# A graph network in one kernel: message terms as the weights of the source sums, and two transfers of the first layer issued at other places

## The chip, the core and the metric

The kernel runs on one core of a Trainium2 chip. The core has five engines with instruction streams of their own: TensorE (PE, with its weight loads shown as PEld), VectorE (DVE), ScalarE (ACT), GpSimd (POOL) and SyncE (SP), which issues most of the DMA transfers. They wait for one another through semaphores. The metric is device time in microseconds; lower is better.

## What is computed

A graph has 6250 nodes with 128 features and 106250 directed edges, sorted by destination (50000 random pairs in both directions and one loop for each node). The reference, cut to what matters:

```python
h = relu(layernorm(x))
for W_l, W_r, b in layers:                      # two layers
    agg = segment_sum(h[src], dst) / max(count, 1)
    h = relu(agg @ W_l + h @ W_r + b)
x = x + h
h = relu(layernorm(x))                          # third stage
m = relu(concat(h[src], h[dst]) @ W_interact + b_interact)
m = segment_sum(m, src) / 4
out = x + relu((h + m) @ W_update + b_update)   # the last x is the middle sum
```

## The kernel before

**Start, to about 128 us.** The edges are read, the layer norm is made, and 1250 bins of five destination nodes each are filled from the edge list. `t_rows` in DRAM receives the features of all nodes as two float16 terms (a high and a low one, 512 bytes a row).

**First layer, about 128 to 560 us.** The count matrix of edges is built in 16 slabs of 320 destination nodes. One slab has 16 units. For each unit DVE makes two one-hot tiles (L1843, L1848), PE multiplies them into PSUM (`build`, L1244) and ACT evicts the product into one of two slab buffers (L1023). Between the builds of slab s, PE multiplies the feature table with slab s-1 (`dense_part`, L1255). Of the 16 slabs the first 14 (`STORED`) are also written to DRAM for the second layer (SP, L684), and ACT may not evict slab s before the store of slab s-2, which used the same buffer, has landed. `finish` (L1859) on DVE multiplies a slab's sum by the inverse counts of its nodes, which SP has loaded into `inv` (`load_inv`, L669). Beside this run a histogram of the sources, whose sums DVE takes out of PSUM at slab 2, unit 4 (`blocks_counted`, L1893), and the stages of a sort.

The destinations past node 5120 go another way. POOL gathers the source rows of their edges out of `t_rows` with indirect transfers, eight of 128 rows for each of 20 groups (`fetch_tail`, L898). The row buffer holds 20 transfers: from transfer 20 on, each further eight wait until PE has used an earlier group. PE sums a group at its place in the stream of units (`tail_group`, L1313), and DVE multiplies it by inverse counts from `tail_inv` (L1916) and adds the result (L1813).

**Second layer, about 560 to 900 us**, takes the 14 stored slabs back from DRAM and the last two from their buffers.

**Third stage, about 900 to 1538 us.** The edges are now sorted by source in 50 blocks of 125 nodes, each with 18 tiles of 128 edges, in six groups of three tiles (`GB` = 6, `GT` = 3, 300 groups in all). For each group gi:

- POOL gathers the `b_rows` of nine of the 18 tiles of a block (L934, 9 transfers a block, nine buffers `rows_g`, so up to nine groups ahead);
- DVE makes one-hot tiles three groups ahead (`prepare`, L2215, L2225, L2228);
- PE sums each tile's source and destination part in PSUM bank gi % 4 (`edge_sum`, L1470 and L1479; each is a weight load of 128 columns and a matmul of 128 columns);
- DVE adds the gathered rows into the bank (`add_rows`, L2261);
- ACT writes relu of it as the float16 high term of `msg` (L1155), DVE the low term (`low_term`, L2269);
- four groups later PE sums the messages into their source nodes (`source_sum`, L1490): the one-hot of the sources, 128 edges by 126 columns, is the weights, and both terms of the messages, 256 columns, stream past it. The result of a block is 126 by 256 in PSUM bank 4 + b % 2.

After a block, DVE adds the two halves (`whole_sum`, L2277), PE transposes the sum (`turn_sum`, L1502) and DVE scales it and adds it to `hT` (`keep_sum`, L2283). After every five or so blocks PE multiplies by the update weights (L1510), DVE adds bias and residual (L2290, L2297), and SP stores the output.

**Order around the change.** Everything is in program order on each engine. In the loop over gi, PE runs `source_sum(gi - 4)`, `edge_sum(gi)`, then at group 2 of block b `turn_sum(b - 2)`. DVE runs `add_rows(gi)`, `low_term(gi - 1)`, `prepare(gi + 3)`, then at group 2 `split_lo` and `keep_sum(b - 2)`, at group 4 `whole_sum(b - 1)`. On SP's queue the order was: store of `t_rows[0]` (L656), the fill of `a_rows` with `x` from DRAM to DRAM (L658: 6250 rows of 512 bytes, 125 rows a step, only so that every row is defined before the gathers of the third stage), then for each slab s: at s = 4 `load_tail_inv(0)` (L661), `load_inv(0, s)`, the wait for the eviction of slab s, the store of slab s.

Of the kernel before, what the change touches and what calls it, by code (L numbers as in the profile page):

```python
# [6 lines left out]
def gnn_kernel(nc, x, src, dst, W_l0, W_r0, b0, W_l1, W_r1, b1, W_int, b_int, W_upd, b_upd, out):  # L7
# [5 lines left out]
    ALU = mybir.AluOpType  # L13
    ACT = mybir.ActivationFunctionType
    AX = mybir.AxisListType
    P = 128
    N, D = x.shape
# [34 lines left out]
    STORED = NS - 2  # L52
# [11 lines left out]
    HALVES = 2  # L64
# [16 lines left out]
    BN = 125  # L81
    NB = N // BN
    BE = BN + 1
# [8 lines left out]
    GB = 2 * SIDE  # L92
    GT = TB // GB
# [100 lines left out]
    LAST_BLOCK = [min((c + 1) * CT * P, N) - 1 for c in range(NC)]  # L194
    LAST_BLOCK = [node // BN for node in LAST_BLOCK]
# [7 lines left out]
    with ctx:  # L203
        start = {}
# [8 lines left out]
        def sem(name):  # L213
            return ctx.enter_context(nc.semaphore(name))

        a_rows = nc.dram_tensor("a_rows", [N, D], f32).ap()
# [25 lines left out]
        settle = sb("settle", [P, 1])  # L242
# [28 lines left out]
        ident = sb("ident", [P, P])  # L271
# [11 lines left out]
        scaled = sb("scaled", [P, SC])  # L283
# [5 lines left out]
        ps = ctx.enter_context(nc.psum_tensor("ps", [P, 8, 512], f32))  # L289
# [76 lines left out]
        msg = [x.bitcast(f16).rearrange("p (j k f) -> p j k f", j=GT, k=2) for x in msg_f]  # L366
# [22 lines left out]
        src_hot = [x.bitcast(f16)[:, 0:GT * BE].rearrange("p (j n) -> p j n", j=GT) for x in src_hot_f]  # L389
# [8 lines left out]
        g_b = inv[:, 1, 0:D]  # L398
        g_msg = scaled[:, 0:D]
        g_hot = scaled[:, D:D + BN]  # L400
        block_sum = scaled[:, 0:D]

        s_const = sem("s_const")
        s_iota = sem("s_iota")
# [50 lines left out]
        s_first = sem("s_first")  # L455
# [43 lines left out]
        e_full = sem("e_full")  # L499
        e_msg = sem("e_msg")  # L500
        e_low = sem("e_low")
        e_whole = sem("e_whole")
        e_turned = sem("e_turned")
        e_psum = sem("e_psum")
        e_added = sem("e_added")
        o_lin = sem("o_lin")
        o_biased = sem("o_biased")
# [61 lines left out]
        DECODED_AT = (3, 2)  # L569
# [61 lines left out]
        def _(sp):  # L631
# [13 lines left out]
            for p0, p1 in LAST_ROWS:  # L645
# [9 lines left out]
            sp.wait_ge(PS_[0]["t_lo"], NC)  # L655
            sp.dma_start(t_rows[0].rearrange("(t p) f -> p t f", p=P), table.rearrange("p t k n -> p t (k n)")  # L656
                         ).then_inc(l_store[0], 16)
            sp.dma_start(a_rows.rearrange("(t p) f -> p t f", p=BN), x.rearrange("(t p) f -> p t f", p=BN)  # L658
                         ).then_inc(s_first, 16)
            def load_tail_inv(L):  # L660
                sp.dma_start(tail_inv[L], inv_row[DENSE:ROWS].rearrange("(a n) -> a n", a=1  # L661
                                                                        ).to_broadcast([P, ROWS - DENSE])
# [2 lines left out]
            def load_inv(L, q):  # L665
                if q > 1:
                    sp.wait_ge(AS[L]["scaled"], q - 1)
                s = ORDER[q] if L else q
                sp.dma_start(inv[:, q % 2, :], inv_row[s * SC:(s + 1) * SC].rearrange("(a n) -> a n", a=1  # L669
                                                                                    ).to_broadcast([P, SC])  # L670
                             ).then_inc(s_inv[q % 2], 16)
# [3 lines left out]
                sp.dma_start(slab_rows(slab[q % 2])[:, g, :], slabs_d[ORDER[q], g, :, :]).then_inc(s_land[q % 2][g // 2], 16)  # L675

            for s in range(NS):
                if s == DECODED_AT[0] + 1:
                    sp.wait_ge(AS[0]["hot"], DECODED_AT[0] * SU + DECODED_AT[1] + 2)
                    load_tail_inv(0)  # L680
                load_inv(0, s)
                sp.wait_ge(AS[0]["evict"], min(s * SU + SU, UNITS) + PRE)
                if s < STORED:
                    sp.dma_start(slabs_d[s].rearrange("g p n -> p g n"), slab_rows(slab[s % 2])  # L684
                                 ).then_inc(s_kept[s % 2], 16)
            sp.wait_ge(q_build, BUILT)
            sp.wait_ge(s_irow, 32)
            load_tail_inv(1)
# [53 lines left out]
            for c in range(NC):  # L742
                sp.wait_ge(f_bok, c + 1)
                to = b_rows[c * CB:(c + 1) * CB, :].rearrange("(t p) f -> p t f", p=BN)
# [418 lines left out]
        def _(pe):  # L1163
            t = nc.tensor
# [10 lines left out]
            for h in range(2):  # L1175
                last = t.matmul(ps[:, 4, h * HG:(h + 1) * HG], ones[0:HG, :], diag[:, h, :], start=True, stop=True)
# [31 lines left out]
            for k in range(2):  # L1208
                last = t.matmul(ps[:, 5, 0:1], scaled[:, k * D:(k + 1) * D], ones[:, 0:1], start=k == 0, stop=k == 1)
# [14 lines left out]
            with pe.Fori(0, rounds) as r:  # L1224
                pe.wait_ge(c_five, r + 1)
                for k in range(BW):
                    for j in range(NC):
                        last = t.matmul(ps[:, 4, j * BW + k:j * BW + k + 1], five[:, k, j * P:(j + 1) * P],
                                        ones_b[:, 0:1], start=True, stop=True)
# [253 lines left out]
            def source_sum(gi):  # L1483
                b, g = divmod(gi, GB)
                pe.wait_ge(e_low, gi + 1)
                pe.wait_ge(e_dvehot if g in DVE_HOTS else e_srchot, hots(gi))
                if g == 0 and b > 1:
                    pe.wait_ge(e_whole, b - 1)
                for j in range(GT):
                    last = t.matmul(ps[0:BE, 4 + b % 2, 0:2 * D], src_hot[gi % 6][:, j, :],  # L1490
                                    msg[gi % 3][:, j, :, :].rearrange("p k f -> p (k f)"),
                                    start=g == 0 and j == 0, stop=g == GB - 1 and j == GT - 1)
                last.then_inc(e_psum, 1)

            def turn_sum(b):
                pe.wait_ge(e_whole, b + 1)
                if b:
                    pe.wait_ge(e_added, b)
                updated = sum(last < b for last in LAST_BLOCK)
                if updated:  # L1500
                    pe.wait_ge(o_biased, updated)
                t.transpose(ps[:, 7, 2 * P:2 * P + BN], block_sum[0:BN, :], ident[0:BN, 0:BN]).then_inc(e_turned, 1)  # L1502

            def update(c):
                pe.wait_ge(e_added, LAST_BLOCK[c] + 1)
# [8 lines left out]
            for gi in range(NGR):  # L1514
                b, g = divmod(gi, GB)
                if gi > 3:
                    source_sum(gi - 4)
                edge_sum(gi)
                if gi == GENERAL_AT + AHEAD:
                    general_edges()  # L1520
                if g == 2 and b > 1:
                    turn_sum(b - 2)
                if g == GB - 1 and b - 2 in LAST_BLOCK:
                    update(LAST_BLOCK.index(b - 2))
            turn_sum(NB - 2)
            source_sum(NGR - 4)
            source_sum(NGR - 3)
            source_sum(NGR - 2)
            source_sum(NGR - 1)
            turn_sum(NB - 1)  # L1530
            update(NC - 1)

        @block.vector
        def _(dve):
            v = nc.vector
# [35 lines left out]
            for h in range(2):  # L1571
# [5 lines left out]
                                 op=ALU.min, axis=AX.X))  # L1577
            nc.vector.sem_inc(k_flag, 1)
            dve.wait_ge(s_x[1], 48)
            for t in range(4 * CT, NT):  # L1580
                last = tile_stats(x0, t)
# [44 lines left out]
            def floor_div(to, of, temp):  # L1626
# [9 lines left out]
                                 in1=gbin[:, 1, :].unsqueeze(2).to_broadcast([P, NW, WT]), op=ALU.subtract))  # L1636
            v.tensor_reduce(out=met[:, 0, :], in_=k_rel.rearrange("p (k t) -> p t k", t=WT)[:, :, 0:NW - 1],
                            op=ALU.min, axis=AX.X)
            link(v.tensor_reduce(out=met[:, 1, :], in_=k_rel.rearrange("p (k t) -> p t k", t=WT), op=ALU.max,
                                 axis=AX.X))  # L1640
            link(v.tensor_tensor(out=met[:, 0, 0:WT - 1], in0=met[:, 0, 0:WT - 1], in1=rel_of[:, NW - 1, 0:WT - 1],
                                 op=ALU.min))
# [620 lines left out]

            def low_term(gi):
                dve.wait_ge(e_msg, gi + 1)
                if gi > 2:
                    dve.wait_ge(e_psum, gi - 2)
                to = msg[gi % 3]
                v.scalar_tensor_tensor(out=to[:, :, 1, :],  # L2269
                                       in0=ps[:, gi % 4, 0:GW].rearrange("p (j f) -> p j f", j=GT), scalar=0.0,  # L2270
                                       in1=to[:, :, 0, :], op0=ALU.max, op1=ALU.subtract).then_inc(e_low, 1)

            def whole_sum(b):
                dve.wait_ge(e_psum, (b + 1) * GB)
                if b:
                    dve.wait_ge(e_turned, b)
                v.tensor_reduce(out=block_sum[0:BN, :], in_=ps[0:BN, 4 + b % 2, 0:2 * D].rearrange("p (k f) -> p f k", k=2),  # L2277
                                op=ALU.add, axis=AX.X).then_inc(e_whole, 1)

            def keep_sum(b):  # L2280
                dve.wait_ge(e_turned, b + 1)
                to = hT[:, b * BN:(b + 1) * BN]
                v.scalar_tensor_tensor(out=to, in0=ps[:, 7, 2 * P:2 * P + BN], scalar=settle[:, 0:1], in1=to,  # L2283
                                       op0=ALU.mult, op1=ALU.add).then_inc(e_added, 1)

            def biased(c):
# [17 lines left out]
            for gi in range(NGR):  # L2304
                b, g = divmod(gi, GB)
                add_rows(gi)
                if gi:
                    low_term(gi - 1)
                if gi + AHEAD < NGR:
                    prepare(gi + AHEAD)  # L2310
                    source_hot(gi + AHEAD)
                if gi == GENERAL_AT:
                    general_edges()
                if g == 2 and b + 1 < NB:
                    split_lo(b + 1)
                if g == 2 and b > 1:
                    keep_sum(b - 2)
                if g == 4 and b:
                    whole_sum(b - 1)
                if g == GB - 1 and b - 2 in LAST_BLOCK:  # L2320
                    biased(LAST_BLOCK.index(b - 2))
                if g == 1 and b - 3 in LAST_BLOCK:
                    residual(LAST_BLOCK.index(b - 3))
            low_term(NGR - 1)
            keep_sum(NB - 2)
            whole_sum(NB - 1)
            keep_sum(NB - 1)
            biased(NC - 1)
            residual(NC - 1)
# [22 lines left out]
```

## Time and profile before

| | us |
|---|---|
| median of three runs | 1537.74 (1535.6 to 1540.89) |
| the profiled execution | 1539.85 |
| its span in the profile | 1538.0 |

| engine | busy us | share of the span |
|---|---|---|
| PE | 1326.8 | 86% |
| DVE | 1322.1 | 86% |
| ACT | 939.7 | 61% |
| POOL | 931.3 | 61% |

The shares are averages over stages that have different limits. The profiled execution is 1.85 us longer than its span, and 2.1 us above the median. "Idle" in a row is the time for which the engine did nothing just before the instruction, with what released it. Successive DVE instructions overlap by some hundredths of a microsecond, so the price of one in a dense stream is the distance from its start to the next start, not its duration.

### The profile page before, as it was taken

To read this page: it belongs to the slowest core of one execution; us is meant where nothing else is said; L and a number is where in the kernel's file an instruction comes from. 1 tells how busy PE (TensorE), PEld (TensorE's weight loads), DVE (VectorE), ACT (ScalarE), POOL (GpSimd) and SP (SyncE) were. 2 spreads that over 40 slices of the span, in tenths; PEclk is the share of its full clock that TensorE was granted. 3 is DMA by queue.
4 is the path that set the end of the run, shared out by engine and by line. 5 is a ranking of instruction groups with operands and counts; after the bars stand their busy time and mean duration, and the time that the engine had idled before them with its cause. 6 is when DMAs were issued, how large, how long until landed. Compare 5 with 4: busy or idle time off the path is not lost.

```text
span 1538.0 us, 39495 instructions
## 1 busy us (share of the span) xinstructions
PE 1326.8 (86%) x14762; PEld 1131.1 (74%) x14762; DVE 1322.1 (86%) x3949; ACT 939.7 (61%) x1831; POOL 931.3 (61%) x942
## 2 busy tenths in 40 slices
PE   1426788998999988999999679899999999999997
PEld 1213566776777866777777578889899999998887
DVE  7948797999999845777776779999999999999998
ACT  2646576787778940101001458888878878888886
POOL 5263505887882006677770157777777777777773
PEclk9955899999999999999999789999999999999999
DMA  4005724646473238899996134444445444444542
GB/s 122 0 1 139 287 110 158 242 170 244 154 260 136 103 95 281 279 301 311 301 285 220 30 98 126 120 128 128 121 127 126 124 144 123 131 122 128 128 120 62
DMA packets 121784, 241.62 MB, mean 157 GB/s; under 512 B 20184, under 2 KB 74601, under 8 KB 121594
## 3 DMA queue, kind: packets, MB, share of 16 engines
q1 hardware_dynamic: 95179, 187.74, 36.8%
q0 software_dynamic: 24832, 50.78, 13.5%
q8 instruction: 118, 1.93, 0.5%
q10 hardware_dynamic: 1584, 0.59, 0.2%
q14 instruction: 71, 0.58, 0.1%
HBM read 169.09 MB, written 73.14 MB: 157 GB/s over the span
## 4 chain that ended last, share of the span: by engine, by line
PE 50%; DVE 31%; issue 7%; ACT 4%; DMA 3%; POOL 2%; SPq 1%; ACTq 0%; DVEq 0%; POOLq 0%
PE ps L1273 13%; PE ps L1479 12%; PE ps L1255 6%; DVE room L2225 6%; DVE hot L1848 4%; PE ps L1244 4%; PE ps L1490 3%; PE ps L1470 3%; DVE slab L2269 2%; PE ps L1313 2%; DVE ps L2261 2%; DVE keys L1974 2%; DVE hot L1843 2%; DVE keys L1973 2%; DVE slab L2225 1%
## 5 line engine op out<-in xcount | busy, mean ns | idle before, releaser
L1023 ACT ACTIVATE slab<-ps 128x980 f16<-128x980 f32 x256 | 321.4, 1277 | 111.9 <-PE ps L1244 94.6
L934 POOL DMA_INDIRECT cells<-b_rows,work x236 | 243.3, 1031 | 74.9 <-issue 68.0
L1479 PE MATMUL ps<-slab,room 125*128 125x128 f16 x3538 | 236.0, 221 | 35.2 <-DVE room L2225 32.7
L1255 PE MATMUL ps<-slab,room 128*128 128x320 f16 x1568 | 251.9, 301 | 0.1
L1134 ACT ACTIVATE lnw<-iota_w,keys 128x126 f32<-128x126 f32 x750 | 242.5, 389 | 0.0
L1479 PEld LDWEIGHTS ps<-slab,room 125*128 125x128 f16 x3538 | 206.5, 98 | 48.7 <-DVE room L2225 48.3
L1470 PE MATMUL ps<-inv,hot 125*128 125x128 f16 x1800 | 224.2, 220 | 5.1 <-DVE hot L2215 4.9
L1273 PE MATMUL ps<-slab,room 128*128 128x320 f16 x1568 | 227.1, 301 | 0.0
L1244 PE MATMUL ps<-hot 128*128 128x245 bf16 x1024 | 161.4, 283 | 50.3 <-DVE hot L1848 38.0
L898 POOL DMA_INDIRECT hot<-t_rows,pairs x160 | 165.9, 1037 | 55.4 <-issue 48.2
L1273 PEld LDWEIGHTS ps<-slab,room 128*128 128x128 f16 x1568 | 153.4, 98 | 59.6 <-issue 2.7
L1255 PEld LDWEIGHTS ps<-slab,room 128*128 128x128 f16 x1568 | 153.5, 98 | 47.4 <-issue 1.0
L1479 PE MATMUL ps<-slab 125*128 125x128 f16 x2676 | 179.6, 220 | 2.7 <-DVE slab L2225 2.6
L898 POOL DMA_INDIRECT tslot<-t_rows,pairs x80 | 117.2, 1465 | 95.6 <-PE ps L1313 62.4
L1244 PEld LDWEIGHTS ps<-hot 128*128 128x128 bf16 x1024 | 108.1, 116 | 86.9 <-DVE hot L1848 51.5
L1848 DVE TENSOR_TENSOR hot<-iota_hi,cell_hi 128x984 bf16<-128x984 bf16 x256 | 170.7, 667 | 0.0
L1479 PEld LDWEIGHTS ps<-slab 125*128 125x128 f16 x2676 | 157.0, 98 | 3.8 <-DVE slab L2225 3.5
L1470 PEld LDWEIGHTS ps<-inv,hot 125*128 125x128 f16 x1800 | 144.1, 98 | 10.2 <-issue 5.0
L1973 DVE TENSOR_TENSOR keys<-keys 128x256 f32<-128x256 f32 (+1 forms) x212 | 112.0, 528 | 38.4 <-ACT keys L1006 22.5
L934 POOL DMA_INDIRECT cell_lo<-b_rows,work x115 | 119.8, 1042 | 36.3 <-issue 33.5
L934 POOL DMA_INDIRECT cell_hi<-b_rows,work x99 | 104.9, 1060 | 31.4 <-issue 28.7
L898 POOL DMA_INDIRECT rest<-t_rows,pairs x80 | 104.0, 1300 | 24.9 <-issue 24.1
(376 smaller groups left out, 2418.7 us busy)
## 6 DMA issues: line engine op xcount, KB each, us to landing
slabs_d<-slab SPq DMA_DIRECT2D x14, 3920.0 KB
slab<-slabs_d SPq DMA_DIRECT2D x98, 560.0 KB, 5.3
hot<-lane_d SPq DMA_DIRECT2D x50, 576.0 KB
inv<-inv_row SPq DMA_DIRECT2D x32, 160.0 KB, 6.6
keys<-up_d SPq DMA_DIRECT2D x25, 160.0 KB
room<-up_d SPq DMA_DIRECT2D x25, 160.0 KB
cells<-b_rows,work POOLq DMA_INDIRECT x236
t_rows<-room SPq DMA_DIRECT2D x1, 3200.0 KB, 13.6
```

The source lines that it names most:

```text
L898: p.indirect_dma_start(tail_rows[L][i % RT[L]], None, t_rows[L], bass.IndirectOffsetOnAxis(ap=pairs[:, t, 0:1], axis=0)).then_inc(e_gath[a ...
L934: p.indirect_dma_start(rows_g[gi % RS][:, j, :], None, b_rows, bass.IndirectOffsetOnAxis(ap=node_t[:, t:t + 1], axis=0)).then_inc(e_gath[g ...
L1023: a.activation(slab[par][:, :, u * UB * BW:(u + 1) * UB * BW].rearrange("p h (k d) -> p k h d", k=UB), psum_unit(u).rearrange("p k (h d) - ...
L1134: last = a.activation(far[:, j, :], iota_w[:, 0:BE], ACT.Square, bias=lane_g[:, gi * GT + j:gi * GT + j + 1])
L1244: last = t.matmul(to[:, k, :], lo[:, :, k], hi[:, k, 0:HB], start=True, stop=True)
L1255: last = t.matmul(ps[:, 4 + s % 2, 0:SC], table[:, h, term, :], slab[s % 2][:, h, :], start=k == 0, stop=k == HI * HALVES - 1)
L1273: last = t.matmul(ps[:, 4 + q % 2, 0:SC], table[:, h, term, :], slab[q % 2][:, h, :], start=k == 0, stop=k == HI * HALVES - 1)
L1470: last = t.matmul(to, lanes_of, a_terms[0:BN, b % 2, k, :], start=k == 0, stop=not picked and k == HALVES - 1)
L1479: last = t.matmul(to, end_hot[g // 3][0:BN, u:u + P], bt[0:BN, bt_at(tile, w), k, :], start=False, stop=w == w1 - 1 and k == HALVES - 1)
L1848: v.tensor_tensor(out=hot[:, u % 4, P * UB:(P + HB + 1) * UB].rearrange("p (k w t) -> p k w t", k=UB, t=2), in0=iota_hi[:, :].rearrange("p ...
L1973: v.tensor_tensor(out=new[0], in0=old[0], in1=old[1], op=ALU.max if down else ALU.min)
L2225: last = v.tensor_scalar(to, row, (down_s if h else up_s)[0:BN, w:w + 1], None, ALU.is_equal)
```

## The change

In the third stage the operands of the source sum change places. A message term, 128 edges by 128 features, is the weights, and the one-hot of the sources, 125 columns, streams past it. High and low term go one after the other into the same PSUM columns, so there are six matmuls for a group of three tiles instead of three, and the block's sum comes out as features by nodes, with the two terms already added. `whole_sum`, `turn_sum`, their semaphores and the buffer `block_sum` go. `keep_sum(b)` reads the sum where it is; it stands where `whole_sum` stood (group 4 of block b + 1). `low_term` no longer waits for the source sum three groups back on its own; ACT, whose high term it waits for, still does.

In the first layer the fill of `a_rows` moves from ahead of the slabs to slab 14, behind the wait for that slab's eviction. `load_tail_inv(0)`, which stood ahead of `load_inv(0, 4)`, stands behind `load_inv(0, 3)` and its own wait for slab 3, unit 3, and so ahead of the wait for slab 3's eviction and of its store.

```diff
             sp.wait_ge(PS_[0]["t_lo"], NC)
             sp.dma_start(t_rows[0]. ...).then_inc(l_store[0], 16)
-            sp.dma_start(a_rows.rearrange("(t p) f -> p t f", p=BN), x.rearrange("(t p) f -> p t f", p=BN)
-                         ).then_inc(s_first, 16)
...
             for s in range(NS):
-                if s == DECODED_AT[0] + 1:
+                load_inv(0, s)
+                if s == DECODED_AT[0]:
                     sp.wait_ge(AS[0]["hot"], DECODED_AT[0] * SU + DECODED_AT[1] + 2)
                     load_tail_inv(0)
-                load_inv(0, s)
                 sp.wait_ge(AS[0]["evict"], min(s * SU + SU, UNITS) + PRE)
                 if s < STORED:
                     sp.dma_start(slabs_d[s]. ...).then_inc(s_kept[s % 2], 16)
+                if s == STORED:
+                    sp.dma_start(a_rows.rearrange("(t p) f -> p t f", p=BN), x.rearrange("(t p) f -> p t f", p=BN)
+                                 ).then_inc(s_first, 16)
...
                 if g == 0 and b > 1:
-                    pe.wait_ge(e_whole, b - 1)
+                    pe.wait_ge(e_added, b - 1)
                 for j in range(GT):
-                    last = t.matmul(ps[0:BE, 4 + b % 2, 0:2 * D], src_hot[gi % 6][:, j, :],
-                                    msg[gi % 3][:, j, :, :].rearrange("p k f -> p (k f)"),
-                                    start=g == 0 and j == 0, stop=g == GB - 1 and j == GT - 1)
+                    for k in range(HALVES):
+                        last = t.matmul(ps[:, 4 + b % 2, 0:BN], msg[gi % 3][:, j, k, :], src_hot[gi % 6][:, j, 0:BN],
+                                        start=g == 0 and j == 0 and k == 0,
+                                        stop=g == GB - 1 and j == GT - 1 and k == HALVES - 1)
                 last.then_inc(e_psum, 1)
-            def turn_sum(b):
...
-                t.transpose(ps[:, 7, 2 * P:2 * P + BN], block_sum[0:BN, :], ident[0:BN, 0:BN]).then_inc(e_turned, 1)
...
                 dve.wait_ge(e_msg, gi + 1)
-                if gi > 2:
-                    dve.wait_ge(e_psum, gi - 2)
...
-            def whole_sum(b):
+            def keep_sum(b):
                 dve.wait_ge(e_psum, (b + 1) * GB)
-                if b:
-                    dve.wait_ge(e_turned, b)
-                v.tensor_reduce(out=block_sum[0:BN, :], ...).then_inc(e_whole, 1)
-
-            def keep_sum(b):
-                dve.wait_ge(e_turned, b + 1)
                 to = hT[:, b * BN:(b + 1) * BN]
-                v.scalar_tensor_tensor(out=to, in0=ps[:, 7, 2 * P:2 * P + BN], scalar=settle[:, 0:1], in1=to,
+                v.scalar_tensor_tensor(out=to, in0=ps[:, 4 + b % 2, 0:BN], scalar=settle[:, 0:1], in1=to,
                                        op0=ALU.mult, op1=ALU.add).then_inc(e_added, 1)
...
-                if g == 2 and b > 1:
-                    keep_sum(b - 2)
                 if g == 4 and b:
-                    whole_sum(b - 1)
+                    keep_sum(b - 1)
```

## Rows read from the trace of the kernel before

**Rows 1.** Busy time by engine: us, PE, PEld, DVE, ACT, POOL, PEclk, DMA, GB/s.

```profile
1064.00:1416.00 352.00, 333.60 (x5231) 322.49 (x5228) 350.66 (x1278) 284.08 (x758) 272.75 (x261) 1.00 0.48 127
```

**Rows 2.** Timeline of SP's queue, first layer: start, us, line, transfer.

```profile
125.31 9.47 SPq L658 DMA_DIRECT2D a_rows<-in_x  x1
134.83 33.27 SPq L669 DMA_DIRECT2D inv<-inv_row  x1
```

**Rows 3.** Timeline at the eviction of slab 2; in brackets the idle time ahead.

```profile
182.00 3.67 ACT L1023 ACTIVATE slab<-ps 128x980 f16<-128x980 f32 x3 [9.22 <-DMA slabs_d<-slab]
...
183.40 0.98 PE L1244 MATMUL ps<-hot 128*128 128x245 bf16 x4 [7.68 <-ACT slab L1023]
...
187.42 1.28 DVE L1893 TENSOR_REDUCE share<-ps 128x32 f32<-128x512 f32 x2 [10.03 <-PE ps L1351]
```

**Rows 4.** Timeline at the first tail group of the first layer.

```profile
235.15 0.57 SPq L661 DMA_DIRECT2D cells<-inv_row  x1
...
249.47 0.29 DVE L1916 TENSOR_TENSOR hrow<-ps,cells 128x128 f32<-128x128 f32 x1 [6.22 <-DMA cells<-inv_row]
...
258.32 0.35 DVE L1813 SCALAR_TENSOR_TENSOR hT<-ps,lift,hT 128x128 f32<-128x128 f32 x1 [2.21 <-PE ps L1319]
```

**Rows 5.** Timeline of the tail's gathers on POOL, and PE's use of group 8.

```profile
235.91 3.66 POOL L898 DMA_INDIRECT tslot<-t_rows,pairs  x1 [56.86 <-PE ps L1313]
...
257.09 0.94 POOL L898 DMA_INDIRECT tslot<-t_rows,pairs  x1 [5.51 <-PE ps L1313]
...
339.70 0.95 POOL L898 DMA_INDIRECT rest<-t_rows,pairs  x1 [0.30 <-issue]
...
342.77 0.83 PE L1313 MATMUL ps<-hrow,tslot 128*128 128x128 f16 x12
```

**Rows 6.** DMA queue, 138 to 150 us: packets, MB, share; timeline, layer one's end.

```profile
q1 hardware_dynamic: 2256, 1.15, 32.1%
...
517.50 2.66 ACT L1023 ACTIVATE slab<-ps 128x980 f16<-128x980 f32 x2
...
557.99 0.49 DVE L1859 TENSOR_TENSOR scaled<-ps,inv 128x320 f32<-128x320 f32 x1
```

**Rows 7.** Chain that ended last, one block; a group: busy us, mean ns.

```profile
1219.90 1.00 PE ps L1479 x18
1221.02 0.33 PE ps L1490 x3
...
1222.69 0.12 PE ps L1502
...
L1490 PEld LDWEIGHTS ps<-slab,rest 128*126 128x126 f16 x288 | 31.7, 137 | 1.8 <-DVE slab L2269 1.8
```

**Rows 8.** Timeline of one block of the third stage, PE and DVE.

```profile
1224.98 0.28 PE L1470 MATMUL ps<-inv,hot 125*128 125x128 f16 x2
...
1225.50 0.29 DVE L2261 TENSOR_TENSOR ps<-ps,cells 128x128 f32<-128x128 f32 x1
...
1230.94 0.41 DVE L2277 TENSOR_REDUCE scaled<-ps 125x128 f32<-125x256 f32 x1
...
1231.28 0.42 DVE L2261 TENSOR_TENSOR ps<-ps,cells 128x256 f32<-128x256 f32 x1
```

**Rows 9.** Timeline: gathers of group 0 in blocks 10 and 42, and their use.

```profile
1028.13 1.45 POOL L934 DMA_INDIRECT cell_hi<-b_rows,work  x1 [0.30 <-issue]
...
1033.41 0.30 DVE L2261 TENSOR_TENSOR ps<-ps,cell_hi 128x128 f32<-128x128 f32 x1
...
1416.47 0.94 POOL L934 DMA_INDIRECT cells<-b_rows,work  x1 [0.30 <-issue]
...
1432.34 0.28 DVE L2261 TENSOR_TENSOR ps<-ps,cells 128x128 f32<-128x128 f32 x1
```

**Rows 10.** Timeline of the third stage's end.

```profile
1530.25 0.42 DVE L2277 TENSOR_REDUCE scaled<-ps 125x128 f32<-125x256 f32 x1 [0.38 <-PE ps L1490]
...
1531.10 0.35 DVE L2283 SCALAR_TENSOR_TENSOR hT<-ps,settle,hT 128x125 f32<-128x125 f32 x1 [0.42 <-PE ps L1502]
```

More of the change, by code:

```diff
@@ L400, in gnn_kernel @@
         g_hot = scaled[:, D:D + BN]
-        block_sum = scaled[:, 0:D]
         s_const = sem("s_const")
@@ L501, in gnn_kernel @@
         e_low = sem("e_low")
-        e_whole = sem("e_whole")
-        e_turned = sem("e_turned")
         e_psum = sem("e_psum")
@@ L1487, in source_sum @@
                 if g == 0 and b > 1:
-                    pe.wait_ge(e_whole, b - 1)
+                    pe.wait_ge(e_added, b - 1)
                 for j in range(GT):
-                    last = t.matmul(ps[0:BE, 4 + b % 2, 0:2 * D], src_hot[gi % 6][:, j, :],
-                                    msg[gi % 3][:, j, :, :].rearrange("p k f -> p (k f)"),
-                                    start=g == 0 and j == 0, stop=g == GB - 1 and j == GT - 1)
+                    for k in range(HALVES):
+                        last = t.matmul(ps[:, 4 + b % 2, 0:BN], msg[gi % 3][:, j, k, :], src_hot[gi % 6][:, j, 0:BN],
+                                        start=g == 0 and j == 0 and k == 0,
+                                        stop=g == GB - 1 and j == GT - 1 and k == HALVES - 1)
                 last.then_inc(e_psum, 1)
-            def turn_sum(b):
-                pe.wait_ge(e_whole, b + 1)
-                if b:
[L1498 to L1501, printed above, removed]
-                t.transpose(ps[:, 7, 2 * P:2 * P + BN], block_sum[0:BN, :], ident[0:BN, 0:BN]).then_inc(e_turned, 1)
             def update(c):
@@ L1520, in _ @@
                     general_edges()
-                if g == 2 and b > 1:
-                    turn_sum(b - 2)
                 if g == GB - 1 and b - 2 in LAST_BLOCK:
                     update(LAST_BLOCK.index(b - 2))
-            turn_sum(NB - 2)
             source_sum(NGR - 4)
@@ L1529, in _ @@
             source_sum(NGR - 1)
-            turn_sum(NB - 1)
             update(NC - 1)
@@ L2271, in low_term @@
                                        in1=to[:, :, 0, :], op0=ALU.max, op1=ALU.subtract).then_inc(e_low, 1)
-            def whole_sum(b):
+            def keep_sum(b):
                 dve.wait_ge(e_psum, (b + 1) * GB)
-                if b:
-                    dve.wait_ge(e_turned, b)
-                v.tensor_reduce(out=block_sum[0:BN, :], in_=ps[0:BN, 4 + b % 2, 0:2 * D].rearrange("p (k f) -> p f k", k=2),
-                                op=ALU.add, axis=AX.X).then_inc(e_whole, 1)
-            def keep_sum(b):
-                dve.wait_ge(e_turned, b + 1)
                 to = hT[:, b * BN:(b + 1) * BN]
-                v.scalar_tensor_tensor(out=to, in0=ps[:, 7, 2 * P:2 * P + BN], scalar=settle[:, 0:1], in1=to,
+                v.scalar_tensor_tensor(out=to, in0=ps[:, 4 + b % 2, 0:BN], scalar=settle[:, 0:1], in1=to,
                                        op0=ALU.mult, op1=ALU.add).then_inc(e_added, 1)
@@ L2315, in _ @@
                     split_lo(b + 1)
-                if g == 2 and b > 1:
-                    keep_sum(b - 2)
                 if g == 4 and b:
-                    whole_sum(b - 1)
+                    keep_sum(b - 1)
                 if g == GB - 1 and b - 2 in LAST_BLOCK:
@@ L2324, in _ @@
             low_term(NGR - 1)
-            keep_sum(NB - 2)
-            whole_sum(NB - 1)
             keep_sum(NB - 1)
```

## The prediction, made before the changed kernel ran

> **What bounds the kernel now.** I read busy time by stretch first, then the timeline at the longest waits, then how far each producer runs ahead of its user.
>
> In the middle of the third stage DVE is busy for 350.66 of 352 us and PE for 333.60, so DVE has the least room [rows 1]. POOL looks idle there, 272.75 us of 352, but it issued 261 gathers, and ahead of each stand 0.30 us of issue that aren't counted as busy [rows 1, 9]. 261 times 0.30 is 78, and 273 + 78 is 351 of 352 us: POOL has no room either. Two rows 32 blocks apart give the paces. POOL's first gather of a block starts at 1028.13 in block 10 and at 1416.47 in block 42, 12.14 us a block; DVE's use of it starts at 1033.41 and 1432.34, 12.47 us a block [rows 9]. So POOL's lead grows from 5.3 us to 15.9. The 5.3 us hold the gather's 1.45 us of issue and its landing; up to about block 12 DVE is fed just in time, and only after that is DVE alone the bound.
>
> In the first layer two waits stand out. ACT can't evict slab 2 for 9.22 us, because the store of slab 0 hasn't landed; PE waits 7.68 us behind ACT, and DVE 10.03 us behind PE [rows 3]. The store is late because SP could not issue it: the fill of `a_rows` held SP for 9.47 us, and the load of `inv` behind it for 33.27, until 168.10 [rows 2]. Later DVE waits 6.22 us for `tail_inv`, issued only at 235.15, and 2.21 us more for a PE that had stood still meanwhile [rows 4].
>
> **The change part by part.** *The fill leaves the front.* Without it SP issues the store of slab 0 when the slab is evicted, about 20 us before 168, and it lands before slab 2 asks. `inv`, moved ahead with it, is needed only from slab 2 on. The wait of 9.22 us goes. Between 7.68 (PE's wait) and 10.03 (DVE's) I take 9, nearer to DVE, which works without a gap behind it.
>
> *`tail_inv` earlier.* Its issue moves ahead of the eviction of slab 3, by about a slab (some 20 us). What it is moved past, that eviction's wait and the store of slab 3, isn't held up, since its own wait (slab 3, unit 3) ends long before. DVE's 6.22 us go, and with them the 2.21 of the follow-up: 8.4, at least 6.2. Together 17.4 us.
>
> *What is late next: the tail's gathers.* The gather released by PE's group 0 starts at 235.91; eight take until 251.6 (257.09 less 5.51 of waiting for PE's group 1), and then the stream runs on nearly without a wait to the last gather of group 8, which ends at 340.65, only 2.1 us before PE uses it at 342.77 [rows 5]. With group 0 earlier by 9, its eight gathers end at about 242.6; group 1, earlier by 17, would release the next at about 239, so they follow at once, at 242.9 in place of 257.09. The stream moves by about 14.5, PE wants 17.4, and the 2.1 us are hardly more than a landing. So the first layer gains about 15, not 17.4. Bounds: 18.4 (10.03 + 8.4, gathers keeping up), and about 7.7, if longer gathers beside the slab stores eat half.
>
> *The fill at its new place.* Slab 14's eviction ends at 520.16 [rows 6]. While the fill was alone on SP's queue, that queue moved 1.15 MB in 12 us [rows 6]; 3.2 MB take 33 us, so it ends near 554. Queued behind it on SP are `load_inv(0, 15)`, `load_tail_inv(1)` and the first loads of layer two. The first is the earliest needed: DVE multiplies slab 15 at 557.99 [rows 6]. About 4 us of cover; price 0. Without the cover: the old fill kept SP until 42.8 us after its issue at 125.31 [rows 2], which would be 563.0 here, 5 us late plus a landing, so 8 us at most.
>
> *The source sum on PE.* 18 matmuls with 256 columns a block become 36 with 125. Today three take 0.33 us [rows 7]. Their like in size is the pair of L1479, a load of 128 columns and a matmul of 128: 18 take 1.00 us, 0.056 each [rows 7]. Six are 0.33: PE neither gains nor loses. Below: six at 0.052 (125 of 128 columns) save 0.02 us a group. Above: a pair costs as much as one of today's, 0.11 us. I take 0.056, nearest in shape. The Trainium skill (TensorE: Matmul & The Clock Gate, section Back-to-back issue gap) speaks against the change: in a stream of weight loads and matmuls with 128 columns it puts about 81 ns on each. This trace's 18 in 1.00 us disagree. By the skill's figure the stage would gain almost nothing (third rival).
>
> *`whole_sum` and `turn_sum`.* DVE's slot of L2277 is 0.34 us (1230.94 to the next start at 1231.28) [rows 8], and L1502 holds PE for 0.12 [rows 7]; both go once a block. `keep_sum` keeps its price and moves to the place of `whole_sum`. DVE 12.47 less 0.34 is 12.13, just POOL's 12.14: from block 10 to 42 the lead stays at 5 us instead of growing by 10.6, and that is the gain, with 7 more blocks of 0.34 (2.4): 13. The first ten blocks stay fed by POOL and give nothing. Gathers land unevenly, and a lead that no longer grows can't swallow that; I take off 2: 11. Bounds: 17 (50 times 0.34, POOL no limit) and 8.
>
> *Does PE hold DVE back?* At group 3 PE's sum ends at 1225.26 and DVE uses it at 1225.50: 0.24 us of room [rows 8]. DVE becomes 0.34 faster; the loop from DVE's one-hots over PE back to this point becomes 0.12 faster by L1502. 0.24 + 0.12 - 0.34 leaves 0.02. PE just follows.
>
> *The waits.* `keep_sum(b)` waits for the sum that `whole_sum(b)` waited for, at the same place. `source_sum` at group 0 now waits for `keep_sum` where it waited for `whole_sum`, so the same instruction slot on DVE. The update's wait for `keep_sum` comes a block earlier. `low_term`'s dropped wait was already met by ACT's. All nothing.
>
> *The end.* Behind the last source sum stood L2277 and the transpose; now `keep_sum` can start at 1530.25 in place of 1531.10 [rows 10]: 0.85. With 0.3 for L2277 in the last group, about 1.
>
> **Sum.** 15 + 11 + 1 = 27. Span 1538.0 to 1511, the profiled execution 1539.85 to 1513, the median 1537.74 to 1511.
>
> **Rivals.** *Gathers limit neither stage.* [...] Against: 351 of 352 us. 17.4 + 17 + 1: 1502.
>
> *The gathers take most of the first layer's gain.* For: 2.1 us of lead at group 8. 7.7 + 11 + 1: 1518.
>
> *Pairs with messages as weights cost more than L1479's.* Twelve pairs of two source sums lie in PE's loop between its wait for DVE and group 3. At 0.08 the loop gets 0.29 longer, and of 0.34 a block about 0.05 stays, 2.5 us in all: 15 + 2.5 + 1, 1519. At 0.11 it gets 0.65 longer and costs 0.3 a block: the first layer's gain is gone, 1537. Against: L1479's rows. The skill's 81 ns named above is the milder case.
>
> *The fill at slab 14 isn't covered.* 8 us later than forecast: 1519. For: only 4 us of cover. Against: less other traffic there than in its old place.
>
> *The slower side: the load isn't hidden.* The weights are now the tile written last, `low_term`'s output. If each load, 137 ns for L1490 today [rows 7], stood unhidden ahead of its matmul, the loop's twelve pairs cost 1.64 us more; less the 0.36 of room and transpose, 1.3 a block, 64 in all, against 16 gained: about 1586. It turns slower than before from about 0.11 us a pair on. Against: only the first of a group's six loads waits for a semaphore, and L1479's loads, behind waits on DVE as well, are hidden.
>
> That the change doesn't do what it says is in the third and fifth: DVE's instruction surely goes, and the question is who takes its place.
>
> **How the numbers follow.** Measurement can tell about 0.3% from no change, 4.6 us. Forecast 1511 (1506 to 1516) 0.55; gathers no limit, 1502, 0.12; gathers eat the first layer, 1518, 0.11; fill uncovered, 1519, 0.09; dearer pairs, 1519 to 1537, 0.08, of which 0.03 end near no change; unhidden loads, 1586, 0.03; nothing moves, 0.02. Faster 0.92, same 0.05, slower 0.03. The range 1502 to 1522 takes in the first four.
>
> **What would show it.** Fill: no wait of ACT on `slabs_d`, and SP's long issue at about 500 instead of 135; the multiplication of slab 15 without a wait on `inv`. `tail_inv`: no wait at L1916. Gathers: PE waiting at tail group 8. Source sum: six matmuls in 0.33 us. Third stage: POOL's lead near 5 us at block 42 instead of 15.9, DVE with short waits for gathers throughout, no L2277 and no transpose. I am wrong in a step if PE waits more for DVE than before at L1479 while DVE waits for L1470 (the pairs), or if POOL's pace leaves 12.1 us a block.

## The result, and the profile after

The changed kernel takes 1517.12 us (median of four runs, 1513.23 to 1523.65) where the kernel before takes 1539.32 beside it: 0.985 of before, 95% interval 0.982 to 0.987, which is 24 us less (the two medians differ by 22). The forecast was 27 us less, 1511, with 1502 to 1522 as its range. In a later set of five runs the same kernel stood at 0.983 (0.981 to 0.985). The profiled execution has a span of 1511.4 us against 1538.0, 26.6 less.

The total was near, but its parts were not. Putting the same instruction of both traces side by side, DVE is 17.3 us earlier behind the two stalls, 19.5 from the tenth tail group on, 18.6 at the start of the third stage, 24.8 at its last block and 26.6 at the end. So the first layer gave about 19 (15 forecast), the third stage 6.2 (11 forecast) and the end 1.8 (1 forecast).

First SP's queue in the changed kernel: start, us held, line, transfer. It answers [rows 2] and [rows 6].

```profile
124.12 9.49 SPq L664 DMA_DIRECT2D inv<-inv_row  x1
147.44 0.36 SPq L679 DMA_DIRECT2D slabs_d<-slab  x1
...
500.70 0.93 SPq L682 DMA_DIRECT2D a_rows<-in_x  x1
502.21 27.82 SPq L664 DMA_DIRECT2D inv<-inv_row  x1
530.14 0.35 SPq L656 DMA_DIRECT2D work<-inv_row  x1
```

The store of slab 0 is issued at 147.44 in place of 168.16. The transfer issued behind the fill holds SP's queue for 27.82 us in the new place, as the one behind it did for 33.27 in the old one. The 9.47 us that the prediction gives to the fill were not the fill's: the load of `inv`, which now stands in that place behind the store of `t_rows`, is held for 9.49.

The timeline at the eviction of slab 2, at the first tail group, at tail group 9, and at the multiplication of slab 15 (in brackets the idle time ahead); it answers [rows 3], [rows 4] and [rows 6].

```profile
174.15 3.75 ACT L1021 ACTIVATE slab<-ps 128x980 f16<-128x980 f32 x3 [0.91 <-PE ps L1242]
178.16 1.28 DVE L1879 TENSOR_REDUCE share<-ps 128x32 f32<-128x512 f32 x2 [0.32 <-PE ps L1349]
...
233.91 0.28 DVE L1902 TENSOR_TENSOR hrow<-ps,cells 128x128 f32<-128x128 f32 x1
241.01 0.35 DVE L1799 SCALAR_TENSOR_TENSOR hT<-ps,lift,hT 128x128 f32<-128x128 f32 x1 [0.47 <-PE ps L1317]
...
339.20 1.06 PE L1311 MATMUL ps<-hrow,rest 128*128 128x128 f16 x16
...
538.51 0.49 DVE L1845 TENSOR_TENSOR scaled<-ps,inv 128x320 f32<-128x320 f32 x1
```

ACT's 9.22 us, DVE's 10.03 and 6.22 are gone. Slab 15 is multiplied at 538.51, 38 us behind the issue of the fill and without a wait. The row at 339.20 has a counterpart that the prediction left out. In the kernel before, PE waited 2.02 us ahead of tail group 9:

```profile
358.66 1.05 PE L1313 MATMUL ps<-hrow,rest 128*128 128x128 f16 x16 [2.02 <-issue]
```

The profile puts this wait down to nothing. The eighth gather of group 9 left POOL at 351.92, and by the records of its semaphore its last part landed at 358.57, just ahead of PE: the gathers came last there.

Next, one group of the source sum on PE, in the timeline:

```profile
1214.76 0.50 PE L1489 MATMUL ps<-tslot,slab 128*128 128x125 f16 x6
1215.10 0.28 PE L1468 MATMUL ps<-inv,hot 125*128 125x128 f16 x2
```

Six matmuls of the new form take 0.34 us to the next start, as three of the old form did [rows 7].

Busy time in the middle of the third stage (columns as in [rows 1]):

```profile
1042.00:1394.00 352.00, 334.07 (x5756) 325.30 (x5754) 345.17 (x1258) 286.24 (x766) 271.29 (x264) 1.00 0.46 129
```

and the waits of DVE in the same stretch (us in total, times, longest):

```profile
DVE slab L2253 <- ACT slab L1153: 7.0, 23, 0.5
```

DVE is busy for 345.17 of 352 us, where it was 350.66 [rows 1]: it has less to do and stands still for more. Its one recorded wait is that of `low_term` (L2253) for ACT's high term (L1153), 23 times in 28 blocks, 0.30 us each. The kernel before has 0.4 us of it in a stretch of the same length. The timeline of one block shows where it stands:

```profile
1208.72 0.42 DVE L2247 TENSOR_TENSOR ps<-ps,cells 128x256 f32<-128x256 f32 x1
...
1209.18 0.49 ACT L1153 ACTIVATE slab<-ps 128x384 f16<-128x384 f32 x1 [0.49 <-DVE ps L2247]
...
1214.96 0.30 DVE L2247 TENSOR_TENSOR ps<-ps,cell_hi 128x128 f32<-128x128 f32 x1
1215.06 0.47 ACT L1153 ACTIVATE slab<-ps 128x384 f16<-128x384 f32 x1
1215.56 0.56 DVE L2253 SCALAR_TENSOR_TENSOR slab<-ps,slab 128x384 f16<-128x384 f32 x1 [0.30 <-ACT slab L1153]
...
1218.87 0.49 ACT L1153 ACTIVATE work<-ps 128x384 f16<-128x384 f32 x1 [1.45 <-DVE ps L2247]
1220.68 0.34 DVE L2260 SCALAR_TENSOR_TENSOR hT<-ps,settle,hT 128x125 f32<-128x125 f32 x1
1220.93 0.42 DVE L2247 TENSOR_TENSOR ps<-ps,cell_lo 128x256 f32<-128x256 f32 x1
```

A block has two halves. From `add_rows` of group 5 (1208.72) to `low_term` of group 2 (1215.56) ACT works without a break from 1209.18 on: it evicts the high terms of four groups, and between them it makes one-hots and a split. That half takes 6.84 us. From there to the next `add_rows` of group 5 (1220.93) ACT has idle time (1.45 us here), and DVE alone sets the pace: 5.37 us. The two `low_term` of the kernel before, around its `add_rows` of group 5 at 1231.28 [rows 8]:

```profile
1225.87 0.56 DVE L2269 SCALAR_TENSOR_TENSOR slab<-ps,slab 128x384 f16<-128x384 f32 x1
...
1238.11 0.56 DVE L2269 SCALAR_TENSOR_TENSOR slab<-ps,slab 128x384 f16<-128x384 f32 x1
```

Its second half took 5.41 us, and its first 6.83, as long as now. So ACT set the pace of the first half already. DVE's wait for it was short: `low_term` started 0.37 us behind the start of `add_rows` (1225.50), where 0.20 is usual in this trace behind an `add_rows` of that size, and the view of waits leaves out gaps as short as the 0.08 us that were left between the two.

Before, `keep_sum` stood in the first half and `whole_sum` in the second. Now `keep_sum` stands in the second, where it takes the place of `whole_sum` (0.25 us to the next start, in place of 0.34). The first half got no shorter, since ACT's run didn't: DVE waits there for longer, 0.60 us from start to start, and 0.30 of it are now seen as a hole.

Last, POOL's first gather of blocks 10 and 42 and DVE's use of it, the rows that answer [rows 9]:

```profile
1007.27 1.49 POOL L932 DMA_INDIRECT cell_hi<-b_rows,work  x1 [0.30 <-issue]
...
1012.64 0.29 DVE L2247 TENSOR_TENSOR ps<-ps,cell_hi 128x128 f32<-128x128 f32 x1
...
1392.55 0.94 POOL L932 DMA_INDIRECT cells<-b_rows,work  x1 [0.30 <-issue]
...
1408.27 0.29 DVE L2247 TENSOR_TENSOR ps<-ps,cells 128x128 f32<-128x128 f32 x1
```

DVE's pace is 12.36 us a block (395.63 by 32), not 12.13; POOL's is 12.04, not 12.14; and the lead still grows, from 5.4 to 15.7 us.

### The profile page after: what moved, and what is told of

Read it like the earlier page. It is cut to its first block, busy times and chain, and to the rows that moved or that the text cites. A ratio compares the mean times of both kernels' runs of the same rounds, so it can differ in the third digit from the quotient of the medians.

```text
span 1511.4 us, 40749 instructions
## 1 busy us (share of the span) xinstructions
PE 1318.1 (87%) x15612; PEld 1129.9 (75%) x15612; DVE 1307.1 (86%) x3899; ACT 939.7 (62%) x1831; POOL 922.8 (61%) x942
## 4 chain that ended last, share of the span: by engine, by line
DVE 38%; PE 35%; ACT 12%; issue 10%; DMA 2%; SPq 1%; POOL 1%; ACTq 0%; DVEq 0%; POOLq 0%
PE ps L1271 13%; DVE room L2211 7%; ACT lnw L1132 6%; PE ps L1253 6%; DVE hot L1834 5%; PE ps L1242 4%; PE ps L1477 3%; DVE ps L2247 3%; DVE hot L2201 2%; DVE hot L1829 2%; DVE slab L2253 2%; PE ps L1311 2%; DVE keys L1960 2%; DVE keys L1959 2%; ACT slab L1153 1%
## 5 line engine op out<-in xcount | busy, mean ns | idle before, releaser
L932 POOL DMA_INDIRECT cells<-b_rows,work x236 | 239.7, 1016 | 74.8 <-issue 68.9
L896 POOL DMA_INDIRECT tslot<-t_rows,pairs x80 | 107.9, 1349 | 86.8 <-PE ps L1311 54.1
L1468 PEld LDWEIGHTS ps<-inv,hot 125*128 125x128 f16 x1800 | 132.2, 98 | 5.2 <-issue 5.0
L896 POOL DMA_INDIRECT rest<-t_rows,pairs x80 | 111.2, 1390 | 24.4 <-issue 24.4
```

Source lines behind the costliest of these rows:

```text
L896: p.indirect_dma_start(tail_rows[L][i % RT[L]], None, t_rows[L], bass.IndirectOffsetOnAxis(ap=pairs[:, t, 0:1], axis=0)).then_inc(e_gath[a ...
L932: p.indirect_dma_start(rows_g[gi % RS][:, j, :], None, b_rows, bass.IndirectOffsetOnAxis(ap=node_t[:, t:t + 1], axis=0)).then_inc(e_gath[g ...
L1468: last = t.matmul(to, lanes_of, a_terms[0:BN, b % 2, k, :], start=k == 0, stop=not picked and k == HALVES - 1)
```

## The experiments

Two theories stood at the start. For the third stage: DVE's saving is given back as a wait for ACT, because `keep_sum` left ACT's unbroken run; against it the prediction's account (POOL's pace) and a third, PE's loop. For the first layer: the tail's gathers take part of the gain, as a stream that moves as a whole; against it, that they have room.

This table is worked out from the traces: the first `add_rows` of the third stage, DVE's and POOL's pace from block 10 to 42, and the median block in that stretch. The ratios to the kernel before have their 95% intervals.

| kernel | first add_rows | DVE's pace | median block | POOL's pace | ratio |
|---|---|---|---|---|---|
| before | 906.6 | 12.47 | 12.27 | 12.14 | |
| changed | 888.0 | 12.36 | 12.25 | 12.04 | 0.985 (0.982 to 0.987) |
| changed, later set | 890.9 | 12.35 | 12.24 | 12.11 | 0.983 (0.981 to 0.985) |
| moves | 887.5 | 12.47 | 12.26 | 12.26 | 0.990 (0.987 to 0.993) |
| tail_only | 903.0 | 12.47 | 12.26 | 12.30 | 0.996 (0.994 to 0.998) |
| fill_only | 894.5 | 12.47 | 12.26 | 12.22 | 0.996 (0.994 to 0.998) |
| src_only | 905.4 | 12.35 | 12.21 | 12.02 | 0.995 (0.993 to 0.997) |
| keep_g1 | 885.1 | 12.17 | 11.96 | 11.91 | 0.980 (0.976 to 0.984) |
| keep_g0 | 886.7 | 12.15 | 11.92 | 11.97 | 0.978 (0.976 to 0.980) |
| keep_late | 902.8 | 13.42 | 12.58 | 13.25 | 1.027 (1.024 to 1.030) |

The two executions of the changed kernel differ by 2.9 us at the first `add_rows` and by 5.6 in the span (1511.4 and 1517.0), but by 0.01 in the pace. The four kernels with the third stage of before (before, `moves`, `tail_only`, `fill_only`) agree to 0.01 as well. So the pace is the sharp measure, and single positions are good to some 3 us.

**The two parts apart.** `moves` is the kernel before with both moved transfers and nothing else; `src_only` is the rest of the change.

```diff
 # moves: the kernel before, with
-            sp.dma_start(a_rows. ...)            # ahead of the slabs
...
+                load_inv(0, s)
+                if s == DECODED_AT[0]:
+                    sp.wait_ge(AS[0]["hot"], ...)
+                    load_tail_inv(0)
...
+                if s == STORED:
+                    sp.dma_start(a_rows. ...)
 # src_only: the changed kernel without these lines, in before's order
```

> The kernel before with the two moved transfers alone; the third stage is as before. If the parts of the change are independent, the first layer keeps what the changed kernel gained there: 18.6 us by the start of the third stage (add_rows at 906.6 in before moves to about 888), pace of the third stage 12.47 us a block as before, time about 0.988 of before. If the third stage's pace also hangs on where the gathers stand when it begins, pace or lead of POOL differ from before and the total is off 18.6 by over 2 us.

> The kernel before with the third stage's part of the change alone; the fill and tail_inv stay in front. Theory now (DVE's saving is given back as a wait of low_term for ACT): the pace of the third stage is 12.36 us a block as in the changed kernel, low_term waits 0.30 us in most blocks, and the kernel gains 6 to 8 us, 0.995 of before. The prediction's account (POOL's pace of 12.14 us is the limit) wants 12.14 a block, a lead of POOL that stays near 5 us, and 12 us, 0.992 of before.

`moves` starts the third stage 19.1 us earlier and keeps before's pace to the hundredth; `src_only` starts it 1.2 earlier and has the changed kernel's pace and its wait. By the ratios the parts are worth 15 and 8 us (give or take 5 and 3), 23 together beside 24 to 26 for the whole, so they are independent as far as these runs can tell. POOL does differ in `moves` (12.26 us a block, and a lead of 11.3 us at block 42), and DVE's pace doesn't follow it. `src_only` answers the first question too: not 12.14, but 12.35, 0.995 and not 0.992.

**The single moves.** `tail_only` and `fill_only` each have one of the two.

> The kernel before with load_tail_inv(0) moved alone; the fill stays in front. Theory of the prediction (the gathers behind PE's first tail groups are a stream that moves as a whole): PE's group 0 stays where it is, so the stream can move by no more than the 5.5 us that POOL waited for PE's group 1; the gain in the first layer is 5.5 us or less, and PE waits for gathers around groups 8 and 9. Rival (the long gathers of 4 to 6 us come whenever, and the stream has room): the 8.4 us go whole, and PE waits for no gather: 8 us or more.

> The kernel before with the fill moved alone; load_tail_inv(0) stays where it was. Both moves together moved the third stage's start by 19.1 us (906.6 to 887.5), tail_inv's alone by 3.6. If the two add up, the fill alone gives 15 us or more. If tail_inv's move is worth 8 us only once the fill's move has released the first gathers earlier (theory now): the fill alone gives 9 to 12 us in the first layer, DVE still waits about 6 us for tail_inv, and the two single moves together give some 6 us less than both at once.

In `tail_only` DVE's wait for `tail_inv` is gone and DVE gains 8.0 us there (its lead goes from 1.3 to 9.4), until PE comes to tail group 3. There it gives back 8.0:

```profile
277.36 1.44 PE L1313 MATMUL ps<-hrow,tslot 128*128 128x128 f16 x12 [5.62 <-issue]
```

Behind this wait stand the gathers of groups 2 and 3. The first is released by PE's group 0 at 234.61, 1.3 us earlier than before, which is no more than DVE's lead of that execution, and four of group 3's take long; the last of group 3 lands at 277.27:

```profile
252.14 4.18 POOL L898 DMA_INDIRECT tslot<-t_rows,pairs  x1 [0.30 <-issue]
256.62 4.91 POOL L898 DMA_INDIRECT tslot<-t_rows,pairs  x1 [0.30 <-issue]
...
264.47 3.46 POOL L898 DMA_INDIRECT tslot<-t_rows,pairs  x1 [0.30 <-issue]
268.23 6.24 POOL L898 DMA_INDIRECT rest<-t_rows,pairs  x1 [0.30 <-issue]
```

So the gathers do limit when `tail_inv` alone comes early, in the one execution that was profiled. In `fill_only` the stall at slab 2 goes (DVE 9.4 us earlier), the wait at group 9 goes (11.2 earlier from there), and `tail_inv` is as late as ever:

```profile
240.23 0.29 DVE L1917 TENSOR_TENSOR hrow<-ps,cells 128x128 f32<-128x128 f32 x1 [6.40 <-DMA cells<-inv_row]
```

At the start of the third stage that is 12.1 us for the fill and 3.6 for `tail_inv`, together 15.7, against 19.1 for both at once. I had expected some 6 us between the two sums and see 3.4, hardly more than the positions are good for. The wait of 2 us at group 9 is gone in both traces, so the 15.7 hold it twice. The executions aren't typical either: the profiled one of `tail_only` is the slowest of its ten (1540.71, median 1536.41), that of `fill_only` the fastest of its eight (1528.17, median 1532.67). By the ratios each move alone gives 6 us, and both 15. What is beyond that scatter are the waits themselves: `tail_inv`'s 8 us are lost at group 3 without the fill's move and kept with it.

**The place of `keep_sum`.** In `keep_g1` and `keep_g0` the changed kernel's `keep_sum` goes back into ACT's run, three or two groups later than it stood.

```diff
-                if g == 4 and b:
-                    keep_sum(b - 1)
+                if g == 1 and b > 1:          # keep_g0: g == 0
+                    keep_sum(b - 2)
...
             low_term(NGR - 1)
+            keep_sum(NB - 2)
             keep_sum(NB - 1)
```

> The changed kernel with keep_sum(b-2) at the end of group 1 in place of keep_sum(b-1) at group 4: the same DVE work, placed in the half of the block in which ACT runs without a break and DVE waits 0.30 us for it. If ACT's run is the limit there: the wait of low_term falls to under 0.1 us, the pace goes from 12.36 to about 12.12 us a block, and the kernel is 11 to 12 us faster than the changed one, about 0.977 of before. If POOL is the limit (its pace in the changed kernel was 12.04): the pace stops above 12.12, its lead falls and DVE waits for gathers. If PE's loop is the limit: pace stays at 12.3 or more, and PE waits less for DVE at L1477.

> The changed kernel with keep_sum(b-2) at the end of group 0: another place inside ACT's unbroken run. If the place inside or outside that run is what counts: 12.17 us a block as with group 1 (keep_g1), no recorded wait of low_term, 0.977 to 0.980 of before. If group 1 helped for another reason (room for PE's group 3 behind it), the pace stays above 12.25.

No DVE work is saved, and the pace falls from 12.36 to 12.17 and 12.15. In `keep_g1` the wait of `low_term` is recorded once in the stretch, with 0.6 us, and DVE is busy nearly throughout:

```profile
DVE slab L2253 <- ACT slab L1153: 0.6, 1, 0.6
```

```profile
1042.00:1394.00 352.00, 338.97 (x5865) 330.76 (x5863) 350.77 (x1277) 293.32 (x783) 270.96 (x267) 1.00 0.47 131
```

A median block takes 11.96 us, 0.31 less than before, nearly the whole slot of L2277. POOL follows at 11.91, and PE does 339 us of work in the stretch where it did 334: neither was the limit. `keep_g0`, set beside the changed kernel in the later set, takes 1505.8 us where that takes 1514.2, 8.4 less, and their intervals don't meet. For `keep_g1` 11 to 12 us less were expected; its interval (0.976 to 0.984) meets the changed kernel's, and that it is faster rests on its pace.

**The reverse, on the kernel before.** `keep_late` moves before's `keep_sum(b - 2)` from group 2 to group 4.

```diff
-                if g == 2 and b > 1:
+                if g == 4 and b > 1:
                     keep_sum(b - 2)
```

> The kernel before with keep_sum(b-2) at group 4, ahead of whole_sum(b-1), in place of group 2: no DVE work is added or taken away. If DVE's total is the limit: 12.47 us a block as before, no change. If ACT's unbroken run from add_rows of group 5 to low_term of group 2 is a limit of its own (6.99 us in the changed kernel): low_term waits about 0.2 us in most blocks, the pace becomes about 12.65, and the kernel is some 9 us slower, 1.006 of before.

The kernel became 41 us slower, not 9. The waits of DVE and PE from 1064 to 1390 show two effects:

```profile
DVE ps L2261 <- PE ps L1470: 13.2, 9, 2.5
DVE slab L2269 <- ACT slab L1155: 7.1, 20, 0.5
...
PE ps L1510 <- DVE hT L2283: 18.3, 5, 3.7
```

`low_term` waits for ACT in 20 blocks, 0.35 us each, and the median block is 0.31 longer with the same DVE work: that is the effect it was made for. The rest I had overlooked. In the blocks with an update PE waits in front of it (L1510) for `keep_sum(b - 2)`, which now comes later: five times in this stretch, 3.7 us each. Those blocks take 14.7 to 17.2 us, the ones behind them 13.2 to 13.9, and they make the mean pace 13.42.

The two halves of a block, worked out from the traces of all five (medians over 32 blocks; first half: `add_rows` of group 5 to `low_term` of group 2; second: from there to the next `add_rows` of group 5):

| kernel | first half | second half | DVE in the second half |
|---|---|---|---|
| before | 6.84 | 5.41 | `whole_sum` |
| changed | 6.84 | 5.33 | `keep_sum` |
| keep_g1 | 6.85 | 5.07 | neither |
| keep_g0 | 6.84 | 5.07 | neither |
| keep_late | 6.84 | 5.67 | both |

The first half is the same in all five, with `keep_sum` in it or without: that is ACT's run. The second changes by what DVE does in it. Of the 0.10 us a block that the changed kernel gained, 0.07 lie there; the rest is in the blocks with an update, whose first half takes 7.9 to 8.0 us in place of 8.0 to 8.2.

**The changed kernel again.**

> The changed kernel itself beside the others on one chip: 0.982 to 0.987 of before, 12.36 us a block; with keep_sum in group 0 or 1 it should stand 8 to 11 us above those.

It came out so: pace 12.35, 0.983, and 8.4 us above `keep_g0` by the medians. `low_term`'s wait is 7.0 us there as well.

## Why the prediction was right or wrong

The range held the time and the sign was right, but two of the sum's terms missed in opposite directions (4 too low, 5 too high), so the total is partly luck.

- *The fill leaves the front*: right. 9 forecast; DVE's gap of 10.03 became 0.32, and DVE gained 9.7 there. Of SP's 42.8 us the first 9.47 were not the fill's (see the load of `inv` at 124.12), which the sum doesn't use.
- *`tail_inv` earlier*: right. 8.4 forecast, 8.1 measured (DVE's lead goes from 9.2 to 17.3 us).
- *The tail's gathers take 2.4 of it*: wrong. The step let the stream of gathers run as long as in before, 235.91 to 340.65. In the changed kernel the same gathers, group 2's fifth to group 8's last, run from 226.66 to 316.32. That is 89.7 us in place of 104.7, with no wait of 5.5 in it and with five gathers of over 2 us in place of nine. It is a stream whose long gathers fall elsewhere in each kernel, and `tail_only` shows them falling badly. The limit was real; its size could not be read off by shifting it.
- *The tightest gather*: wrong by 2. I took group 8, with 2.1 us between issue and use, for the tightest place. Group 9, with 6.7, was the one that already waited, 2.02 us under "issue": a landing, which the lead to the end of the issue doesn't show. The first layer's 4 us above forecast are these 2 and the 2.4. So the rival in which the gathers take most of the gain fell; the one in which they limit neither stage was right about the gathers of the changed kernel and wrong about the price, since in the third stage ACT stood where POOL had been put.
- *The fill at its new place*: right. Price 0, no wait at slab 15. The rival in which it is not covered fell.
- *The source sum on PE*: right. 0.33 forecast, 0.34 measured. So the rivals of dearer pairs and of unhidden loads fell. The Trainium skill puts 81 ns on a pair of that size (TensorE: Matmul & The Clock Gate, Back-to-back issue gap); the trace disagrees, at 0.056 us.
- *DVE's slot and POOL's pace*: the step that failed. DVE's 0.34 us a block was to be capped by POOL at 12.14. POOL ran at 12.04 in the changed kernel and at 11.91 in `keep_g1`, and its lead grew as in before, so 12.14 was not its floor; in the changed kernel it even waited once in the 32 blocks, for 0.83 us, until DVE had freed a buffer. "351 of 352 us busy" described how POOL's gathers fill the time, not what they need. The cap was another, and lower: of 0.34 us a block 0.10 stayed, 3.3 us in 32 blocks where 10.6 were counted and 11 forecast for the stage. Of the stage's 6.2 us, 0.7 came behind those blocks and 2.2 in the first ten, to which the forecast gave nothing and which scatter by more than that (last section).
- *"The waits: all nothing"*: this is where the cap is. `keep_sum` "keeps its price and moves" was right for DVE's total and wrong for the block, since the place that it left lies in ACT's run and the place that it took doesn't. For `low_term`'s wait for ACT the kernel before shows 0.4 us in total, and yet ACT's run set the length of that half already, 6.84 us there as in every kernel since; all that a change of DVE's work could give lay in the other half. Neither the forecast nor a rival named it. `keep_g1`, `keep_g0` and `keep_late` show it from both sides.
- *PE's room of 0.02 us at group 3*: held. PE's sum there ends at 1214.93, and DVE uses it at 1214.96.
- *The end*: 1 forecast, 1.8 measured.

The Trainium skill (Perfetto Trace Analysis, Identifying the Most-Contended Engine) says to take the engine with the highest occupancy first. Here DVE at 350.66 of 352 us was that engine, and taking 0.34 us a block from it gave 0.10, since ACT, at 284, is the limit of the first half of each block. The rows differ from the rule there, and the measurement decides; they agree once `keep_sum` stands in ACT's half.

What stays open: why single gathers take 2.3 to 6.8 us and most others 0.94 to 1.4. No run varied that. The lengths recur (4.12 and 6.25, 4.18 and 4.9 us), and the places change between kernels. That gathers are longer the more other transfers run is not what the kernel before shows: the 160 gathers of its second layer, at 263 GB/s, took 0.94 to 1.45 us each.

## What to carry to other kernels

An engine that is 99% busy over a stage needn't be its limit everywhere: split the loop at the waits, and ask in each part which engine runs without a break. When an instruction moves within a loop at equal cost, look at what its old place was covering. A wait with a total near zero can be the limit already, since a view may leave out short gaps: measure such a stretch from start to start, in both kernels. A producer's lead counts to its landing, and a stream of transfers must not be shifted with its durations kept.

## What the runs showed of the hardware

- The clock of PE came back, and fell, at other moments in executions that were otherwise alike. In the changed kernel's profiled execution it was still 0.50 (1.2 GHz) from 149 to 151 us, where the kernel before had 1.00 (2.4 GHz) from 150 to 152, and it fell to 0.51 from 541 to 543, behind 3 us in which PE was busy for 0.81. In the later execution of the same kernel, whose work lies 0.7 us later there, PE was busy for the same 0.81 us of 3 (last row), and the clock stayed at 1.00: the work was the same, and no run shows what decided. Each of the two took 1.5 us of DVE's lead over the kernel before (from 1.0 to -0.5, and from 19.5 to 18.0); the later execution lost 0.2 and nothing there.

```profile
149.00:151.00 2.00, 2.00 (x10) 1.23 (x9) 1.90 (x5) 0.88 (x1) 2.00 (x1) 0.50 1.03 426
...
538.00:541.00 3.00, 0.81 (x2) 0.30 (x2) 1.60 (x5) 0.51 (x1) 0.00 (x0) 1.00 0.12 38
541.00:543.00 2.00, 1.63 (x7) 1.47 (x8) 0.00 (x0) 1.15 (x3) 0.00 (x0) 0.51 0.08 26
...
538.80:541.80 3.00, 0.81 (x2) 0.30 (x2) 1.51 (x5) 0.60 (x1) 0.00 (x0) 1.00 0.13 41
```

- The first ten blocks of the third stage took 122.8 to 131.6 us in nine traces (`keep_late` left aside), and 124.6 and 126.5 in two executions of the same kernel. DVE's waits for gathers there were 0.8 us in `src_only` (122.8), 3.7 in the kernel before (126.8) and 6.8 in `tail_only` (131.6), so late gathers make up most of the difference; why they are late no run singles out.
